# Windowed attention with a conv block: the projection moved behind the transposes of the probabilities, its sum behind their copy, and the negated layer-norm mean computed on VectorE

## What is computed

```python
q = shuffle_invert(conv3(xw, qw, qb), PD)        # also k, v; xw: windows of the normed image
q = ln(q.reshape(B_, E, L).transpose(0, 2, 1), gq, bq)
...
attn = jnp.einsum('bhqd,bhkd->bhqk', q, k)       # q scaled
attn = jax.nn.softmax(attn + bias[None], axis=-1)
out = jnp.einsum('bhqk,bhkd->bhqd', attn, v)
out = out.transpose(0, 2, 1, 3).reshape(B_, L, E)
out = out @ proj_w.T + proj_b
...
xw = short_cut + out
...
y = xr + conv3(jax.nn.gelu(conv3(xr, c1w, c1b), approximate=False), c2w, c2b)
```

## Time and profile before

| | |
|---|---|
| Time before, median of 3 runs (lowest to highest) | 831.84 us (830.34 to 832.01) |
| The profiled execution's own time | 833.53 us |
| Its span on the profile | 831.7 us |
| TensorE, matmuls | busy 749.4 us (90%) |
| VectorE | busy 659.3 us (79%) |
| ScalarE | busy 603.8 us (73%) |
| GpSimd | busy 491.9 us (59%) |
| Chain that ended last, by engine | TensorE 46%, VectorE 23%, no visible wait 11%, GpSimd 10%, ScalarE 9% |
| Projection matmuls (line 1034) | 64 of them, 36.0 us |
| Negated mean (line 721) | 128 on GpSimd, 30.5 us |

### The profile page before, as it was taken

The page is one execution under the profiler, slowest core; times in us unless marked ns, Lnnn a source line. Parts: engine busy times, 40 slices in busy tenths (PEclk is TensorE's granted clock), DMA queues, the critical chain, the costliest instruction groups (busy, mean ns, idle before and its releaser), DMA issues.

```text
span 831.7 us, 18390 instructions
## 1 busy us (share of the span) xinstructions
PE 749.4 (90%) x5704; PEld 536.1 (64%) x5704; DVE 659.3 (79%) x2141; ACT 603.8 (73%) x1287; POOL 491.9 (59%) x1041
## 2 busy tenths in 40 slices
PE   0479999989899999999899999998989999999988
PEld 0257777767456677766656677776645677776753
DVE  5548888987868888888867888898776888887575
ACT  1388888877567888886737888877747788887840
POOL 5356776763346777765436776775335677776410
PEclk9999999999999999999999999999999999999999
DMA  7111160100112132100111216100011213000002
GB/s 256 58 30 30 31 230 5 53 2 1 58 64 90 36 120 111 58 1 1 59 39 52 71 30 230 58 2 1 7 52 65 96 30 130 0 1 1 2 1 101
DMA packets 17643, 47.00 MB, mean 57 GB/s; under 512 B 2080, under 2 KB 2720, under 8 KB 17568
## 3 DMA queue, kind: packets, MB, share of 16 engines
q1 hardware_dynamic: 17568, 46.09, 16.2%
HBM read 37.69 MB, written 8.39 MB: 55 GB/s over the span
## 4 chain that ended last, share of the span: by engine, by line
PE 46%; DVE 23%; issue 11%; POOL 10%; ACT 9%; DMA 1%; DVEq 0%; SPq 0%; ACTq 0%; POOLq 0%
PE y_ps L1011 11%; PE o_bank L1090 6%; PE s_ps L1065 4%; PE pt_ps L1078 4%; POOL ln_rs L724 4%; DVE h_lo L506 3%; DVE ln_st L542 3%; PE ox_ps L1034 3%; DVE h_hi L503 3%; PE s_ps L1124 3%; ACT qk_n L856 3%; PE ox_ps L1124 3%; PE o_bank L1124 3%; PE pt_ps L1124 3%; PE t_ps L1045 2%
## 5 line engine op out<-in xcount | busy, mean ns | idle before, releaser
L856 ACT ACTIVATE qk_n<-y_ps,ln_nr,ln_rs 128x128 f32<-128x128 f32 x256 | 103.7, 459 | 94.7 <-POOL ln_nr L727 94.0
L737 POOL TENSOR_TENSOR sc<-sc,mx 128x512 f32<-128x512 f32 x128 | 133.7, 1045 | 39.2 <-DVE mx L577 39.2
L1011 PE MATMUL y_ps<-w_hi,x_hi 128*128 128x192 f16 (+1 forms) x512 | 148.4, 290 | 0.0
L1011 PE MATMUL y_ps<-w_hi,x_lo 128*128 128x192 f16 (+1 forms) x512 | 148.1, 289 | 0.0
L1011 PE MATMUL y_ps<-w_lo,x_hi 128*128 128x192 f16 (+1 forms) x512 | 148.0, 289 | 0.0
L562 DVE TENSOR_TENSOR sc<-s_ps,biasS 128x512 f32<-128x512 f32 x128 | 86.8, 678 | 54.9 <-PE s_ps L1065 53.7
L1090 PE MATMUL o_bank<-v_bd,pt 128*128 128x66 f32 x1024 | 129.3, 269 | 0.0
L1090 PEld LDWEIGHTS o_bank<-v_bd,pt 128*128 128x128 f32 x1024 | 125.2, 193 | 0.2
L542 DVE BATCH_NORM_STATS2 ln_st<-y_ps 128x6 f32<-128x128 f32 x384 | 88.9, 287 | 42.9 <-PE y_ps L1011 41.1
L720 POOL TENSOR_TENSOR ln_ve<-ln_mv,eps_y 128x3 f32<-128x3 f32 x128 | 33.8, 264 | 148.2 <-DVE ln_mv L547 148.0
L724 POOL TENSOR_TENSOR ln_rs<-ln_ve,neg_half 128x3 f32<-128x3 f32 x128 | 113.3, 885 | 10.7
(11 more groups left out here) (181 smaller groups left out, 1612.4 us busy)
## 6 DMA issues: line engine op xcount, KB each, us to landing
xs<-in_x_sh_dram SPq DMA_DIRECT2D x32, 576.0 KB, 4.2
xst<-in_x_al_dram SPq DMA_DIRECT2D x16, 512.0 KB, 8.0
xf<-in_x_al_dram SPq DMA_DIRECT2D x32, 256.0 KB, 5.3
out_dram<-xf SPq DMA_DIRECT2D x32, 256.0 KB, 2.0
wst<-in_wqkv_dram SPq DMA_DIRECT2D x1, 768.0 KB, 4.2
w1s<-in_w_dram SPq DMA_DIRECT2D x1, 256.0 KB, 8.8
w2s<-in_w_dram SPq DMA_DIRECT2D x1, 256.0 KB, 8.8
biasS<-in_bias_t_dram SPq DMA_DIRECT2D x1, 256.0 KB, 9.7
```

Of the source, the lines that this page charges most:

```text
L737: pool.tensor_tensor(sc[i % 4][:, :, :, :], sc[i % 4][:, :, :, :], mx[i % 2][:, :, :].unsqueeze(2).to_broadcast([P, HP, TOK, 2]), ALU.subt ...
L856: ins = act.activation(qk_n[j][:, t, :].rearrange("p (h y x) -> p h y x", h=HEADS, y=2), by_head(y_ps[j][:, E * t:E * (t + 1)]), ACT.Identity,
L1011: ins = pe.matmul(y.rearrange("p (t e) -> p t e", t=3)[:, :, cols], xx[r % 2][:, s, a % 2, 2 * TS * (a // 2):2 * TS * (a // 2 + TS)], ww[: ...
```

## The change

Three edits. On TensorE, the projection becomes a function `project`, called behind the transposes of the probabilities and ahead of `o(i-2)`, for i = 7, 11, ..., 31; at i = 35, where no such transposes are left, it stays where it was. On VectorE, the sum of the projection onto `xr` stands behind the copy of the transposed probabilities, no longer ahead of the maximum. And the negated mean `ln_nm` is computed by VectorE right behind `ln_mv`, with a wait for `ln_mv` and a new semaphore `ln_negated`; GpSimd's `ln_nr` waits for it.

```diff
@@ VectorE, step
                     ins.then_inc(ln_moments, 1)
+                    v.wait_ge(ln_moments, p0 + (m + 1))
+                    v.tensor_scalar(ln_nm[m % 2][:, :], ln_mv[m % 2][:, :, 0], -1.0, None, ALU.mult).then_inc(
+                        ln_negated, 1)
...
-                if i % 4 == 3 and i >= 7:
-                    r = (i - 7) // 4
-                    v.wait_ge(proj_done, r0 + (r + 1))
...
-                    v.tensor_tensor(rows, rows, ox_ps[:, :].rearrange("p (w i j) -> p w i j", w=NWIN, i=TS),
-                                    ALU.add).then_inc(xr_added, 1)
                 if has(i):
                     v.wait_ge(biased, p0 + (i + 1))
...
                     v.tensor_copy(pt[m % 2][:, :, :], pt_ps[:, :, :]).then_inc(pt_copied, 1)
+                if i % 4 == 3 and i >= 7:
+                    r = (i - 7) // 4
+                    v.wait_ge(proj_done, r0 + (r + 1))
...
+                    v.tensor_tensor(rows, rows, ox_ps[:, :].rearrange("p (w i j) -> p w i j", w=NWIN, i=TS),
+                                    ALU.add).then_inc(xr_added, 1)
@@ GpSimd, step
-                    pool.tensor_tensor(ln_ve[j][:, :], ln_mv[j][:, :, 1], eps_y[:, :], ALU.add)
-                    pool.tensor_scalar(ln_nm[j][:, :], ln_mv[j][:, :, 0], -1.0, None, ALU.mult).then_inc(
+                    pool.tensor_tensor(ln_ve[j][:, :], ln_mv[j][:, :, 1], eps_y[:, :], ALU.add).then_inc(
                         ln_var_eps, 1)
...
                     pool.wait_ge(ln_pow, p0 + (m + 1))
+                    pool.wait_ge(ln_negated, p0 + (m + 1))
                     pool.tensor_tensor(ln_nr[j][:, :], ln_nm[j][:, :], ln_rs[j][:, :], ALU.mult).then_inc(
                         ln_scales, 1)
@@ TensorE
+            def project(i, r0):
+
+                r = (i - 7) // 4
+                pe.wait_ge(ot_copied, r0 + (r + 1))
+                pe.matmul(ox_ps[:, :], projg[:, :], ot[r % 2][:, :], start=True, stop=True).then_inc(proj_done, 1)
...
-                if i % 4 == 3 and i >= 7:
-                    r = (i - 7) // 4
-                    pe.wait_ge(ot_copied, r0 + (r + 1))
-                    pe.matmul(ox_ps[:, :], projg[:, :], ot[r % 2][:, :], start=True, stop=True).then_inc(
-                        proj_done, 1)
+                if i == PAIRS + 3:
+                    project(i, r0)
...
                     ins.then_inc(ptr_done, 1)
+
+                if i % 4 == 3 and 7 <= i < PAIRS:
+                    project(i, r0)
 
                 if has(i - 2):
```

More of the change, by code:

```diff
@@ L203, in conv_attention @@
         ln_scales = sem("ln_scales")
+        ln_negated = sem("ln_negated")
         ln_v_scales = sem("ln_v_scales")
@@ L563, in step @@
                                     s_ps[:, :, 0:256], biasS[:, :, :], ALU.add).then_inc(biased, 1)
-                if i % 4 == 3 and i >= 7:
-                    r = (i - 7) // 4
-                    v.wait_ge(proj_done, r0 + (r + 1))
-                    if i == 7:
-                        v.wait_ge(xr_begun, b * 4 + 5)
-                    rows = xr[:, bass.ds((row0 + r) * TS, TS), :].rearrange("p i (w j) -> p w i j", w=NWIN)
-                    v.tensor_tensor(rows, rows, ox_ps[:, :].rearrange("p (w i j) -> p w i j", w=NWIN, i=TS),
-                                    ALU.add).then_inc(xr_added, 1)
                 if has(i):
@@ L584, in step @@
                     v.tensor_copy(pt[m % 2][:, :, :], pt_ps[:, :, :]).then_inc(pt_copied, 1)
+                if i % 4 == 3 and i >= 7:
+                    r = (i - 7) // 4
+                    v.wait_ge(proj_done, r0 + (r + 1))
+                    if i == 7:
+                        v.wait_ge(xr_begun, b * 4 + 5)
+                    rows = xr[:, bass.ds((row0 + r) * TS, TS), :].rearrange("p i (w j) -> p w i j", w=NWIN)
+                    v.tensor_tensor(rows, rows, ox_ps[:, :].rearrange("p (w i j) -> p w i j", w=NWIN, i=TS),
+                                    ALU.add).then_inc(xr_added, 1)
                 if i % 4 == 3 and 2 <= (i + 9) // 4 < NROW:
```

## The result

The changed kernel takes **840.76 us** (median of 4 runs, 837.81 to 840.94) against 831.4 us before: a ratio of **1.0106**, 95% interval 1.0080 to 1.0131. It is slower by 9.4 us; 841.7 had been forecast. The profiled execution took 840.58 us, of which 838.8 is the span.

A forecast was written before the change was run, and what follows sets the result against it. A loop closed through TensorE and ScalarE, with little slack in either, was taken as the bound. Per image 3 x 0.42 + 0.57 + 0.70 = 2.53, four images 10.1, with -0.8 and +0.6 +9.9: 841.7 us, range 836 to 848.

The forecast's parts named there:

- the hole ahead of `t`: TensorE, old place of the projection: t(18) moves only 0.05 us earlier, to 121.65, since it needs qk_n from ScalarE.
- A row: Row of windows behind the projections of steps 7, 11 and 15: 0.42 us longer each, from 0.34 to 0.57.
- the third step: TensorE, third y-to-y step of a row: finds qk_n ready and runs in 4.04 us in place of 4.66.
- The row behind step 19: ScalarE has one more instruction there and did not wait ahead of ot: takes the whole 0.57 us.
- Steps 23 to the next head: End of an image: statistics 1.10 us late, less two layer-norm gains of 0.20, gives 0.70; steps 28 to 31 add 0.
- The head: Each later image head: VectorE's new instruction lies ahead of the last maxima, 0.20 us each, three heads +0.6.
- The sum, costed at nothing: VectorE, sum behind the copy: waits for the projection until about when VectorE gets there; cost 0.
- The start: Ahead of the first full row: four layer-norm gains of 0.20 us, -0.8 (0 to -1.0).
- No change: Rival: half of the projection (0.48 us) hides beside the weight loads of o; 832.9 us, chance 0.07.
- Faster: Rival: 37 layer-norm runs on the path each give 0.20 us, the moved projection costs nothing; 824.3 us, chance 0.07.
- Held up by each other: Rival: ln_nm on VectorE holds GpSimd's ln_ve for 0.15 us, so ln gains only 0.05; 846 us, chance 0.15.
- Nothing absorbed: Rival: the projection costs 0.96 us in each of 24 rows, 23 us in all; 855 us, chance 0.03.

## Why the prediction was right, and where its steps were not

The time and the sign came out, 840.76 for 841.7, and the mechanism, the hole ahead of `t`, is the one that the runs show. That the size came so close is luck: the sum holds errors that cancel, 4.5 us too much for the slower steps and nothing for falls of the clock that took 4.1.

**The hole, its cause and its place: right.** TensorE idles 0.91 us ahead of `t` in the step of the projection, put down to `qk_n`, and no longer two steps later; the statistics two steps behind the projection wait for `y` (0.19). That `qk_n` comes behind `ot` is what makes the hole: with `ot` moved behind the exponential it goes.

**A row, 0.42 forecast, 0.17 to 0.24 measured: two terms mis-sized.** The projection was given the 0.96 us by which it held up `t`. In its new place it holds up `o` by 121.42 - 120.56 = 0.86, and the step from `y` to `y` grows by 6.04 - 5.20 = 0.84. And the layer norm was shortened by more than the 0.20: from `ln_ve` to `ln_nr` it takes 126.48 - 125.28 = 1.20 where before it took 1.45 (from 127.73 to the 129.18 below), 0.25 less: `ln_rs` starts 0.27 behind `ln_ve` in place of 0.49, and itself runs 0.85 in place of 0.89.

```profile
129.18 0.20 POOL L727 TENSOR_TENSOR ln_nr<-ln_nm,ln_rs 128x3 f32<-128x3 f32 x1
```

With both put in, the prediction's own steps give 0.84 - 0.61 = 0.23 on TensorE's side (the third step fell from 4.66 to 4.05, the forecast 0.62), and 0.57 - 0.12 - 0.05 - 0.15 = 0.25 on ScalarE's side. The row is 0.23 longer, so the two sides end together, as the rows show (`ot` starts 0.04 behind TensorE's last transposes and at once behind `k_m`). The row behind step 19 costs 0.31, not 0.57: the same two terms leave 0.40, and the other 0.09 is not accounted for.

**Steps 23 to the next head, 0.70 forecast, +0.49 without a fall** (+0.75 - 1.13 + 0.87). Direction and place right, and the size is off by the same two terms: with them the step gives 0.90 - 0.12 + 0.20 - 2 x 0.25 = 0.48. As it said, the moved projection of step 27 keeps TensorE's work going until about the time at which `t(31)` gets its `qk_n`: the idle time of 0.99 ahead of `t(31)` is gone.

**The head, +0.20 forecast, +0.21.** Right, as is the price of `ln_nm` on VectorE: from the start of `ln_mv` to that of `sc` 125.31 - 124.90 = 0.41, 0.19 more than the 0.22 of before; 0.20 had been taken between 0.10 and 0.31.

**The sum, costed at nothing: 2.3 us when moved alone.** The step asked what waits for the projection and for the exponential. It did not ask what the sum had been hiding: the 0.13 us between two instructions of which the second reads the first. In the whole change the rows hide it again behind the wait for `y`.

**The start, -0.8 forecast: the sign is right, and the size is about 1.0 to 1.5.** The profiled pair has the scores of step 3 in the first image 1.6 us earlier after the change (62.79 against 64.43), but kernels with the same code up to there spread by as much (61.44 and 63.32), so this pair alone can't tell. All twelve traces can: up to that step their kernels differ only in the negated mean. The four with it on GpSimd have these scores at 63.62 to 65.03, the eight with it on VectorE at 61.44 to 63.36. The means lie 1.5 apart, and 1.0 without the two traces (65.03 and 61.44) that have two falls of the clock ahead of that step, or none, where the others have one. With the 6.2 and the 4.1 below, -1.0 gives 9.3, where the medians differ by 9.4.

**Not forecast at all: the clock.** 6.2 us come from the slower steps, where 10.7 had been summed for the same stretch; 4.1 us come from three falls of the clock. The prediction followed the hole through the engines as a delay, and asked of step 27 only whether its projection is late; it did not ask what 1.95 us without work do to TensorE itself. Before, the projection lay in that stretch and split it: TensorE idled 1.13 us ahead of it (the row is of the second image), and the clock stayed at 1.00.

```profile
372.09 1.13 PE L1034 MATMUL ox_ps<-ot,projg 128*128 128x512 f32 x2 [1.13 <-ACT ot L843]
```

The Trainium skill, "TensorE: Matmul & The Clock Gate", section "What's actually happening", has the rule that would have raised the question: the slow clock is the default, and activity releases it. The rows agree, with 0.68 and 0.90 of the clock behind the 1.95 us and 1.00 where transposes had filled a part of it; what decides between a fall and none at the same idle time, no run here shows.

**The rivals.** *No change* needed the projection to hide by half; 0.10 of its 0.96 hid. *Faster* needed TensorE's waits to take the projection; they took 0.61, as forecast, but the part of this rival that concerns the layer norm alone was real: 4.7 us, where it had at most 7.5. *Held up by each other*: `ln_ve` takes 0.19 in the rows beside `ln_nm`, so nothing is held up there. In the heads the long `ln_ve` of 0.61 is gone, and `ln_rs` behind it is held up instead (GpSimd's and VectorE's timelines):

```profile
263.13 0.19 POOL L724 TENSOR_TENSOR ln_ve<-ln_mv,eps_y 128x3 f32<-128x3 f32 x1 [0.59 <-DVE ln_mv L548]
263.40 1.21 POOL L727 TENSOR_TENSOR ln_rs<-ln_ve,neg_half 128x3 f32<-128x3 f32 x1
...
263.16 0.74 DVE L624 SCALAR_TENSOR_TENSOR xf<-xr,x_down,xf 128x512 f32<-128x512 f32 x1
```

The Trainium skill, "SBUF — State Buffer", section "SBUF: two separate sides", which this rival leaned on, agrees with the 1.21 beside VectorE's sum of two tensors in SBUF; for the one-input `ln_nm` on 128 x 3 it had no effect that the trace shows. *Nothing absorbed* fell with the 0.61.

**Which part does what.** The three edits were one change and pull apart: the negated mean gains 4.7 us, the projection and its sum cost 14.6, of which the sum alone is 2.3. The projection's new place fails for what stands ahead of it on ScalarE; with the copies moved and the projection one piece of work further back, the same three edits give 819.46.

## What to carry to other kernels

An instruction that sits in a wait is free there, and its move costs what the wait then leaves open, less what later waits take up; before moving it, find what the wait was for, and move that producer too. Of every instruction that is taken from between two others, ask whether the second reads what the first writes: 0.12 us in a row of windows came to 2.3 us here. And when an edit makes TensorE idle longer in one place, look at the granted clock of the stretch behind it, not only at the delay.

## What the runs showed of the hardware that was not expected

- The granted clock of TensorE fell to its lower level behind 5 of 8 idle times of 1.8 to 2 us and 3 of 16 of 1.3 to 1.45 us, while idle times of 1.5 us one step later, in step 28 (the run with the projection behind `o` and the mean on GpSimd), brought none in four images, and two of 0.66 and 0.76 us close together (the run with the copies behind the exponential) brought one in two images of four. Each fall behind a single idle time cost 1.1 to 1.7 us. Eight unused transposes (1.04 us) in the 1.95 us kept it at 1.00 there, and the median fell by 2.8 us (840.76 to 837.94; the intervals overlap).
- On VectorE a 128x512 maximum started 0.73 us behind the sum whose result it reads, and 0.60 behind an instruction that it does not depend on.
- `ln_rs` on GpSimd, 128x3, takes 0.85 us in place of 0.89 when `ln_nm` does not stand ahead of it on the same engine; why is open.
